# A transformer tower on one core: the last normalisation kept in PSUM with four banks, the first group's choices fetched in two halves, the routes transposed two tiles earlier

## What is computed

```
scores = softmax(x @ wg + bg);  mask = one_hot(top 2 of 16 experts)
route  = scores*mask / (masked scores summed over the 32 sequences + 1e-6) * 32
seq_ids = for each sequence and expert, the 64 positions with the largest route
h   = gelu(x[seq_ids] @ w1[e] + b1[e]);  out = h @ w2[e] + b2[e]
outs = out added back at its positions
z = x + outs
y = (z - mean(z)) / sqrt(var(z) + 1e-5) * gamma + beta;   result = h_tokens + y
```

## Time and profile before

| | us |
|---|---|
| median of 3 runs (lowest, highest) | 600.23 (599.45, 601.31) |
| the profiled execution, its own time | 596.99 |
| its span in the trace | 595.2 |
| PE busy in the span | 518.8 (87%) |
| DVE busy | 486.9 (82%) |
| POOL busy | 395.5 (66%) |
| ACT busy | 357.6 (60%) |
| the last stage, from its first matmul to the end | 395.2 to 595.2 |

### The profile page before, as it was taken

How to read it: one execution, slowest core, us unless ns; L and a number is a source line. 1 busy time by engine, 2 the same in 40 slices (tenths; PEclk the granted TensorE clock), 3 DMA queues, 4 the chain that set the end, 5 groups by cost and what they waited for, 6 DMA issues and landing times. The chain is left out here.

```text
span 595.2 us, 15935 instructions
## 1 busy us (share of the span) xinstructions
PE 518.8 (87%) x5940; PEld 384.1 (65%) x5940; DVE 486.9 (82%) x1001; ACT 357.6 (60%) x752; POOL 395.5 (66%) x537
## 2 busy tenths in 40 slices
PE   4864567999999999999999999659979999999955
PEld 2863334787787778778777776514456776667644
DVE  5487546888888888888888888966876999999996
ACT  2126567787787877877877877325755445555530
POOL 3086003687887877877877878640586667788874
PEclk9695678999999999999999999969989999999979
DMA  6700000000000000000000000000633043053011
GB/s 216 295 2 1 2 1 1 2 4 2 3 4 1 4 3 2 4 2 3 4 3 3 3 2 3 2 1 17 139 70 81 19 114 88 19 123 90 28 36 63
DMA packets 11745, 21.73 MB, mean 37 GB/s; under 512 B 4636, under 2 KB 9748, under 8 KB 9876
## 3 DMA queue, kind: packets, MB, share of 16 engines
q1 hardware_dynamic: 11668, 20.71, 12.6%
HBM read 16.24 MB, written 4.33 MB: 35 GB/s over the span
## 5 line engine op out<-in xcount | busy, mean ns | idle before, releaser
L743 POOL TENSOR_TENSOR s_pl<-s_pf,s_ph 128x512 f16<-128x512 f32 x128 | 146.9, 1159 | 43.7 <-ACT s_ph L821 43.5
L907 DVE TENSOR_REDUCE s_mx<-ps 128x4 f32<-128x512 f32 x128 | 83.8, 677 | 30.2 <-PE ps L1050 30.1
L1469 PE MATMUL ps<-s_w2s,s_hid 128*128 128x256 f16 x768 | 91.8, 278 | 0.0
L815 ACT ACTIVATE s_pf<-ps 128x512 f32<-128x512 f32 x128 | 76.7, 602 | 24.1 <-PE ps L1063 24.1
L1448 PE MATMUL ps<-s_xt_all,s_w1s 128*128 128x512 f16 x384 | 90.2, 388 | 0.5 <-PEq L726 0.5
L1469 PEld LDWEIGHTS ps<-s_w2s,s_hid 128*128 128x128 f16 x768 | 76.8, 100 | 12.4
L821 ACT ACTIVATE s_ph<-s_pf 128x512 f16<-128x512 f32 x128 | 77.5, 637 | 0.0
L1095 PE MATMUL ps<-s_zh,s_cth 128*128 128x256 f16 x256 | 69.8, 273 | 0.0
L1095 PE MATMUL ps<-s_zh,s_ctl 128*128 128x256 f16 x256 | 69.8, 273 | 0.0
L1095 PE MATMUL ps<-s_zl,s_cth 128*128 128x256 f16 x256 | 69.8, 273 | 0.0
L1448 PEld LDWEIGHTS ps<-s_xt_all,s_w1s 128*128 128x128 f16 x384 | 38.2, 100 | 42.4 <-issue 4.5
(11 more groups left out here) (220 smaller groups left out, 1267.8 us busy)
## 6 DMA issues: line engine op xcount, KB each, us to landing
s_rep<-picks SPq DMA_DIRECT2D x16, 512.0 KB, 6.7
s_stage<-in_w SPq DMA_DIRECT2D x2, 1024.0 KB, 13.7
out<-s_ot_a SPq DMA_DIRECT2D x16, 128.0 KB, 1.7
out<-s_lg SPq DMA_DIRECT2D x16, 128.0 KB, 1.7
s_stage<-in_wq SPq DMA_DIRECT2D x1, 1024.0 KB, 4.7
s_stage<-in_wk SPq DMA_DIRECT2D x1, 1024.0 KB, 6.5
s_stage<-in_wv SPq DMA_DIRECT2D x1, 1024.0 KB, 8.1
s_stage<-in_wo SPq DMA_DIRECT2D x1, 1024.0 KB, 9.9
```

The lines of the kernel that those rows point to most:

```text
L743: nc.gpsimd.tensor_tensor(flat(pl[:, b % 2, 4 * j:4 * j + 4, :]), pf[:, j, :], flat(ph[:, b % 2, 4 * j:4 * j + 4, :]), ALU.subtract).then_ ...
L815: nc.scalar.activation(pf[:, j, :], ST[j % 2][:], ACT.Exp).then_inc(exp_done[j], 1)
L907: nc.vector.tensor_reduce(mx[:, b % 2, c:c + 4], A[ab][:].rearrange("p (h k) -> p h k", h=4), AX.X, ALU.max).then_inc(max_done[hf][ab], 1)
L1469: mm = nc.tensor.matmul(ZB[b % 3][:, 0:D], hid[:, g % 2, hp, j, t * P:(t + 1) * P], w2s[:, wp, j, :], start=False, stop=(j == NJ - 1 and h ...
```

## The change

Three edits, in one diff:

1. `stats` and `finish` no longer write to SBUF in between: the sum and the difference from the mean stay in the PSUM bank. The four banks 4 to 7 hold four sequences. `experts_out(b)` now waits until `finish(b - 4)` is done (`o_ok`); the wait for the output tile's store moves from the first instruction of `finish` to the second. Bank 7 also holds the transposed routes, so `experts_out(3)` waits for the copies out of it.
2. `replicas(0)` is four transfers: tiles 0 to 3 for both halves of the partitions, then tiles 4 to 7. The first four masks wait for the first two transfers alone.
3. `routes()` stands behind tile (0, 3) on PE and no longer behind (0, 5).

```diff
-        HB, ZB, RTB = psum[0:NH], psum[4:7], psum[7]
+        HB, ZB, RTB = psum[0:NH], psum[4:8], psum[7]
...
-        zt = zh[:].rearrange("p c n -> p (c n)").bitcast(F32).rearrange("p (r n) -> p r n", n=D)
+        zb = [bank[:, 0:D] for bank in ZB]
...
-                    for h in range(2):
-                        sp.dma_start(rep[h * FP:(h + 1) * FP, g % 2].rearrange("p j t -> p (j t)"),
-                                     picks[g, h].rearrange("(o j) f t -> o (j f t)", o=1).to_broadcast([FP, NJ * GB * S]))\
-                            .then_inc(rep_in[g % 2], 16)
+                    for first, last in ((0, 4), (4, NJ)) if g == 0 else ((0, NJ),):
+                        for h in range(2):
+                            sp.dma_start(rep[h * FP:(h + 1) * FP, g % 2, first:last].rearrange("p j t -> p (j t)"),
+                                         picks[g, h, first:last].rearrange("(o j) f t -> o (j f t)", o=1)
+                                         .to_broadcast([FP, (last - first) * GB * S]))\
+                                .then_inc(rep_first if last == 4 else rep_in[g % 2], 16)
...
-                    dve.wait_ge(rep_in[g % 2], 16 * 2 * (g // 2 + 1))
+                    if g == 0 and j < 4:
+                        dve.wait_ge(rep_first, 16 * 2)
+                    else:
+                        dve.wait_ge(rep_in[g % 2], 16 * 2 * (g // 2 + 1))
...
-                    nc.vector.scalar_tensor_tensor(out=zt[:, b % 4, :], in0=xn[:, b % 2, :], scalar=X_SCALE,
-                                                   in1=ZB[b % 3][:, 0:D], op0=ALU.mult, op1=ALU.add).then_inc(zt_ok, 1)
+                    nc.vector.scalar_tensor_tensor(out=zb[b % 4], in0=xn[:, b % 2, :], scalar=X_SCALE,
+                                                   in1=zb[b % 4], op0=ALU.mult, op1=ALU.add).then_inc(zt_ok, 1)
                     dve.wait_ge(zt_ok, b + 1)
-                    nc.vector.bn_stats(bsz[:, b % 2, :], zt[:, b % 4, :]).then_inc(bsz_ok, 1)
+                    nc.vector.bn_stats(bsz[:, b % 2, :], zb[b % 4]).then_inc(bsz_ok, 1)
...
-                    if b >= 4:
-                        dve.wait_ge(out_st[b % 4], 16 * (b // 4))
-                    nc.vector.scalar_tensor_tensor(out=ot(b), in0=zt[:, b % 4, :], scalar=mvz[:, b % 4, 0:1],
+                    nc.vector.scalar_tensor_tensor(out=zb[b % 4], in0=zb[b % 4], scalar=mvz[:, b % 4, 0:1],
                                                    in1=ga2_b[:], op0=ALU.subtract, op1=ALU.mult).then_inc(zs_ok, 1)
...
-                    nc.vector.scalar_tensor_tensor(out=ot(b), in0=ot(b), scalar=rz[:, b % 4:b % 4 + 1],
+                    if b >= 4:
+                        dve.wait_ge(out_st[b % 4], 16 * (b // 4))
+                    nc.vector.scalar_tensor_tensor(out=ot(b), in0=zb[b % 4], scalar=rz[:, b % 4:b % 4 + 1],
                                                    in1=hb[:, b % 2, :], op0=ALU.mult, op1=ALU.add).then_inc(o_ok, 1)
...
-                    if b >= 3:
-                        pe.wait_ge(zt_ok, b - 2)
+                    if b == 3:
+                        pe.wait_ge(rt_ok, NT)
+                    if b >= 4:
+                        pe.wait_ge(o_ok, b - 3)
...
-                        if (g, j) == (0, 5):
+                        if (g, j) == (0, 3):
                             routes()
```

More of the change, by code:

```diff
@@ L1222, in build @@
                              "chosen_ok"))
+        rep_first = sem("rep_first")
         rep_in = [sem(f"rep_in{n}") for n in range(2)]
@@ L1463, in experts_out @@
                         pe.wait_ge(takes_in, 16 * 4 * (b // 8 + 1))
-                    if b >= 3:
-                        pe.wait_ge(zt_ok, b - 2)
-                    nc.tensor.matmul(ZB[b % 3][:, 0:D], takes[:, b, :], b2s[:], start=True, stop=False)
+                    if b == 3:
+                        pe.wait_ge(rt_ok, NT)
+                    if b >= 4:
+                        pe.wait_ge(o_ok, b - 3)
+                    nc.tensor.matmul(zb[b % 4], takes[:, b, :], b2s[:], start=True, stop=False)
                     for j in range(NJ):
                         for hp, wp in ((0, 0), (0, 1), (1, 0)):
-                            mm = nc.tensor.matmul(ZB[b % 3][:, 0:D], hid[:, g % 2, hp, j, t * P:(t + 1) * P], w2s[:, wp, j, :],
+                            mm = nc.tensor.matmul(zb[b % 4], hid[:, g % 2, hp, j, t * P:(t + 1) * P], w2s[:, wp, j, :],
                                                   start=False, stop=(j == NJ - 1 and hp == 1))
```

## The result

| | before | changed |
|---|---|---|
| median of the timed runs | 600.73 us (599.45 to 601.31, 4 runs) | 585.42 us (582.64 to 586.78, 4 runs) |
| ratio, 95% interval | | 0.9742 (0.9698 to 0.9787) |
| profiled execution, time and span | 596.99, 595.2 | 586.67, 584.8 |
| first matmul of the last stage | 395.22 | 401.22 |
| last stage, to the end of the span | 200.0 | 183.6 |

The two profiled executions differ by only 10.3 us, since the changed one began its last stage 6.0 us later, behind code that is the same. So in what follows the last stage is compared by itself, and times "into the stage" count from its first matmul of hidden tiles.

The account below looks back on a forecast made before the run. DVE, stretched beside POOL, was taken to hold PE back in the last stage. 3.2 + 1.36 + 12.1 + 1.81 - 0.9 - 2.0 = 15.6 us off gave 584.6 us, range 581 to 592.

Parts of the forecast that it names:

- DVE stretched beside POOL bounds the loop: Last stage's loop: DVE's step 5.55 us against PE's mean 4.7, about 1.4 of it stretching; `finish` falls from 2.28 to 1.0.
- 12.1 us of waits and 1.81 us of slow clock: PE's waits from b = 1 to 28, and the slower clock in `experts_out(28)`; both sizes to be gained.
- New waits: `experts_out(b)` needing `finish(b - 4)`: 0.9 us lost over three groups with a round, 2.0 us at the end.
- The start: Routes 2.6 us and halves 2.4 us earlier: first mask at 417.0, `experts_out(0)` at 432.7, 3.2 us earlier.
- The halves: `replicas(0)`: the half set takes 2.4 us off the landing, bounds 0 and 3.3; rival of landing together, chance 0.02.
- The slower clock behind the gap of 3.5 us: First step from `experts_out(0)`: 1.36 us at a slower TensorE go, as the idle gap gets too short.
- The tail: The time behind `stats(31)` to the end of the span: 7.35 us, unchanged.
- fixed cost for a PSUM source: DVE: the page's estimate of 0.065 us more for each of three instructions, 0.2 us a step; not taken into the forecast.

Follow-up runs that it names:

- the second profile: The kernel before, profiled once more with nothing edited; 598.43 us (one run).
- The edit of the loop alone: Edit 1 (normalisation in PSUM with four banks) without edits 2 and 3, on the kernel before; 587.9 us, ratio 0.9801.
- `token` early: On the changed kernel, POOL's `token` two steps earlier, with `hb` in four tiles; 581.47 us, ratio 0.9707.
- the start alone: Edits 2 and 3 (first choices in halves, routes behind tile (0, 3)) on the kernel before; 595.81 us, ratio 0.9953.
- the single edits: Two kernels, each one edit on the kernel before: routes behind tile (0, 3), 597.37 us, ratio 0.9978; `replicas(0)` in halves, 595.97 us, ratio 0.9953.
- both edits of the last kernel: On the changed kernel, `token` two steps earlier and `finish` between the two masks from step 23 on; 586.83 us, ratio 0.9798.

## Why the prediction was right

584.6 us were forecast, 585.42 measured, and the steps can be held against the last stage, which lost 16.4 us in the two profiles (15.6 forecast). Counted from the second profile of the kernel before it is 15.8: 1.65 at the start, 1.67 of slow clock behind it, 11.8 from `experts_out(1)` to (31) and 0.6 in the tail. The mechanism was right; that the sum came out so close is in part luck, since 1.5 us too much for the start stand against 0.8 too little for the loop and 0.6 for the tail, and 0.3 for the first slow clock.

- **DVE stretched beside POOL bounds the loop: right, and shown by intervention.** The edit of the loop alone takes 11.9 us off, and putting one input back in SBUF brings the stretching and, in its profile, 4.1 of the loop's 11.0 to 11.8 us back. For the rest the cause is argued from the durations. `finish` takes 0.48 + 0.48 us as forecast. DVE, busy for 99.8 of 104 us before, is busy for 83.7 now. The step shown is 4.50 us, just over the 3.9 to 4.4 forecast, since two masks take up to 2.28 us and not 1.8.
- **12.1 us of waits and 1.81 us of slow clock can be had: right.** The 1.81 was the low end: `experts_out(28)` took 1.8 to 2.6 us over 2.73 in the five profiles that have the gap of 6.2 us. PE from (1) to (31) takes 131.35 us against 142.3 in the first profile and 143.2 in the second.
- **New waits: the sum right, the places partly.** 0.9 + 2.0 us were forecast. The loop showed none of the 0.9. The end showed 559.23 to 566.99 = 7.76 us for two `experts_out` of 2.73 each, 2.3 us, and some 0.6 more at b = 26. That last wait was not foreseen: `finish(22)` waits for `hb`, and `token` early removes it. What I gave for `experts_out(28)` in the last paragraph, 130 to 131.5 us behind `experts_out(0)`, was a slip: the sum of the text gives 28 x 2.72 + 38 x 1.30 + 2.9 = 128.5, and 566.99 - 438.49 = 128.5 was measured.
- **The start: the mechanism right, the size over.** First mask 21.05 us into the stage (21.8 forecast), `experts_out(0)` 37.3 (37.5 forecast), the masks ahead of the `lo`. But the gain was mis-sized, since the profile that it was counted from had a slow first stretch (a granted clock of 0.70 in its first 10 us, 0.86 in the second profile): 40.67 us into the stage there, 38.92 in two others without the early routes and halves. Counted from those it is 1.65 us, not 3.2. By the first mask, the routes came to 1.6 us (25.0 to 23.4) where 2.6 were forecast, and the halves to 2.5 (25.0 to 22.5) where 2.4 were. To `experts_out(1)`, the clock included, it is 4.75 us against the first profile (forecast 4.56), 3.3 against the second, and 1.65 between the PSUM edit alone and the whole change. The timed runs say 2.8 us for the start alone.
- **The halves:** that the first would land earlier was right (issue to first mask 7.4 us in the second profile, 5.0 with the halves alone); that both edits are needed for masks to run clear of `lo` shows in the three pairs of rows. With the halves there, the routes add 0.4 us (37.66 to 37.25).
- **The slower clock behind the gap of 3.5 us** was taken as sure. It came in both profiles of the kernel before (gaps of 3.50 and 3.32 us) and not behind 3.25 us in the PSUM edit alone, nor behind 1.95 and 2.14 us in the single edits. Behind 6.2 us it came in every profile. What decides is open; that this 1.36 us would go held, but nothing in the first profile made it sure.
- **The tail** was forecast to stay at 7.35 us and was 584.8 - 578.11 = 6.7.
- **The Trainium skill's** fixed cost for a PSUM source (page "VectorE: DVE Perf Modes", section on the TRN2 errata) did not show: the estimate from it was 0.065 us more an instruction, BN_STATS went from 0.428 to 0.432 and the second instruction of `finish` from a minimum of 0.485 to 0.483. The measurement decides. The Trainium skill's page "SBUF — State Buffer", section "Who interferes with whom", says that a DVE instruction with two SBUF inputs contends with a GpSimd instruction that reads SBUF, and one with at most one, outside VectorE's 2-port modes, does not. The two kernels that differ in that input agree with it: 0.484 against up to 1.40 us.

## What to carry to other kernels

When an engine's instruction has a minimum of 0.48 us and a median of 1.26, look for what runs beside it and at which operands never stretch; moving one operand of each to another memory took 1.0 to 1.4 us off a step by the medians, without removing an instruction. A buffer held longer needs one more copy of it: with four banks PE was left with 2.9 us of waits, with three the kernel took 89 us longer. Before an instruction is moved forward to serve one waiter, follow who else stands behind the one it passes: here `normed` and `stats` stood behind the second mask, two engines away.

## What the runs showed that was not expected

- TensorE's clock behind an idle gap was no function of the gap's length alone. Ahead of an `experts_out` it fell from 2.4 to 1.2 GHz behind gaps of 3.50, 3.32 and 2.92 us, and with three banks behind 3.32, 3.23, 2.88, 2.43, 2.42 and even 2.10 us; it did not behind 3.25 us (the PSUM edit alone), 2.66 us (both edits of the last kernel) and 2.62 us (three banks). Behind 5.1 to 6.2 us it always fell. In the kernel with three banks the same gap of 2.10 us was followed by the faster clock at b = 27 and by the slower at b = 29:

```profile
636.90 0.28 PE L1472 MATMUL ps<-s_b2s,s_takes 128*128 128x256 f16 x1 [2.10 <-DVE s_ot_a L1407]
637.01 2.78 PE L1475 MATMUL ps<-s_w2s,s_hid 128*128 128x256 f16 x24
...
646.98 0.40 PE L1472 MATMUL ps<-s_b2s,s_takes 128*128 128x256 f16 x1 [2.10 <-DVE s_lg L1407]
647.17 4.38 PE L1475 MATMUL ps<-s_w2s,s_hid 128*128 128x256 f16 x24
```

With four banks, and in the kernel before, each fall cost 1.4 to 2.6 us in one `experts_out`.
- The same code ahead of the last stage took 394.8 to 401.2 us in the profiles, so a difference of a few us between two single profiles says nothing on a late stage; its own length says more, though that of the kernel before, too, was 200.0 and 199.3 us in its two profiles.
- A first half of a transfer that lands earlier can be of no use while DVE is still busy with the instructions ahead of the mask: with the halves alone the first mask followed without a wait.
